# Turning x tiles 2 to 15 on VectorE from a blocked load, instead of on TensorE

## The chip, the cores and the metric
The kernel runs on one core of a Trainium2 chip. The metric is the device time of one launch in microseconds (us), the median of several runs; lower is better. The five engines are TensorE (PE: matmuls, with PEld for its weight loads), VectorE (DVE), ScalarE (ACT), GpSimd (POOL) and SyncE (SP), which here only issues DMAs. They run side by side and meet at semaphores. Each of them takes its own instructions strictly in the order in which they are written.

## What is computed
Two blocks follow one another on x, of shape (8, 256, 1024) in fp32, that is 16 tiles of 128 tokens by 1024 features:

```python
x = x + ffn0(cond0(x, lang_ids))     # cond0: x @ W0.T + 2 * top-2-gated LoRA (8 experts, rank 16)
                                     # ffn0:  top-1-routed LoRA of cond0's output (8 experts, rank 16)
x = x + ffn1(cond1(x, slot_ids))     # cond1: x @ W1.T + b1 + 2 * LoRA of the slot of each batch
                                     # ffn1:  h @ Wb.T + b_base + 2 * top-2-gated LoRA (8 experts)
```

The kernel never forms the inner activations of the dense products. It folds the weights ahead of time: C0 (1024 x 272) holds all that the first block needs of x, and M = W1.T Wb.T + I (with the routers and LoRA factors of the second block beside it) holds the dense part of the second. Products run in fp32r with each operand split in a high and a low part, so that one product is three matmuls (hi*hi, lo*hi, hi*lo), which the helper `three` issues.

## The kernel before
Up to about 181 us of its trace the kernel prepares: weights are loaded, turned on TensorE, split by ScalarE (high part) and VectorE (low part), and multiplied into C0, D0 and M. The last product there is `m_chunk(K // 2 - 1, 1, 2)`; `m_done` reaches 3 * K when it ends. Only then may `x1T`, `xT_main` and `x1_sums` be written, since they share SBUF with the weights that it reads.

Then come eight slots, b = 0 to 7. Slot b computes the output of tiles m = 2b and m + 1 and, in the same stretch of TensorE's program, the first block for tiles a = 2b + 2 and a + 1 (where there are any). For a tile t of the first block:
- x is loaded (`load_x`: one DMA of 128 rows of 4 KB into `xin`), turned by eight TensorE transposes into two PSUM banks (`turn_x_main`), and split out of PSUM by `xT_part`: ScalarE writes `xThi`, VectorE writes `xTlo`, each in two instructions of 128 x 512.
- `small0(t)` multiplies xT with C0: 24 matmuls of 272 columns. It waits for `xT_lo`, the last of the four splits.
- VectorE's `gates0` works out the top-2 gates and writes `hg`; TensorE turns it (`turn_small(hg_ready, ...)`), ScalarE and VectorE split it, `add_lora0` adds the LoRA. `top1` and `wh` do the same for the router of ffn0. `ffn0(q, g, bank)` multiplies the last factor for both tiles in four quarters of 512 columns.
- `x1_add` forms x1 = ffn0 + x for a quarter: one VectorE add of the bank and `xTlo`, a second one of that sum and `xThi`, into `x1_sums`. `x1T_part` (in the vector program: `split`) splits the quarter into `x1Thi` and `x1Tlo`.

The output of tiles m and m + 1 is 48 "main" steps of three matmuls (x1T by M, 392 columns), which `main_to(n)` advances to step n; between them stand, at steps chosen by hand, the small transposes, `small0`, `add_lora0`, `ffn0`, `lora` and `turn_x_main`. In slot 0 every count of `main_to` is 3 later (`late = 3`). Tiles n = 2b + 4 and n + 1, which the next slot's first block takes, are loaded and turned in slot b: `turn_x_main(n, 0, ...)` after step 40, `turn_x_main(n + 1, 1, ...)` between `lora(m + 1, 1)` and the last `lora(m + 1, 2)`. The next slot begins with `small0(n)`. Slots 0 to 5 have such an n.

VectorE's order at the end of a slot is: `gates1(m + 1)` with the last quarter's add in it, `split(1)`, `wzT_part(m + 1)` (the low part of the turned gates of ffn1, which waits for a TensorE transpose at step 44 and ScalarE's copy of it), `split(2)`, `split(3)`, `xT_part(n)`, `xT_part(n + 1)`, `as_part`. Tiles 0 and 1 are turned during the preparation (`xin_first`, `XT_FIRST`). Tile 2 is turned near its end (`x2_early` into the banks `XT_EARLY`), tile 3 in slot 0, after `adapter(m)`. The slots run unrolled for b = 0, 5, 6, 7 and in a hardware loop for b = 1 to 4.

Of the kernel before, what the change touches and what calls it, by code (L numbers as in the profile page):

```python
# [5 lines left out]
P = 128  # L6
F32 = mybir.dt.float32
# [16 lines left out]
def adaln_ffn(nc, x, lang_ids, slot_ids, W0, Wr0, A0c, B0, route_w, A0f, Bw, W1, b1, lora_As, lora_Bs,  # L24
# [30 lines left out]
    with ctx:  # L55
# [31 lines left out]
        wzThi, wzTlo = sb("wzThi", [P, P], F32R), sb("wzTlo", [P, P], F32R)  # L87

        def gate_tiles(n):
# [18 lines left out]
        with ExitStack() as before_m:  # L108
            sb("below_b_acc", [P, (K - 1) * MW + R], where=before_m)
            b_acc = sb("b_acc", [P, MC], where=before_m)  # L110
            sb("below_x2", [P, (K - 1) * MW + R], where=before_m)
            x2_early = sb("x2_early", [P, D], where=before_m)
        Mhi = sb("Mhi", [P, K, MW], F32R)
# [62 lines left out]
        whT_hi, whT_lo = sem("whT_hi"), sem("whT_lo")  # L176
        x1w_done, x1_half, x1_sum = sem("x1w_done"), sem("x1_half"), sem("x1_sum")
        m_ident, x2_in = sem("m_ident"), sem("x2_in")
        x1T_hi, x1T_lo = sem("x1T_hi"), sem("x1T_lo")
# [89 lines left out]

        XT_BANKS = [(big[1], big[2]), (big[0], big[1])]  # L270
        XT_FIRST = [(pm[0], pm[1]), (pm[2], pm[0])]
        XT_EARLY = (p0, pt)

# [8 lines left out]
        def half_tiles(t, half, h):  # L282
            return t[:, :].rearrange("p (k c) -> p k c", k=K)[:, 4 * h:4 * h + 4, half * P:(half + 1) * P]

        def wait_earlier(eng, s, n):

            if not isinstance(n, int) or n > 0:
                eng.wait_ge(s, n)
# [3 lines left out]
        def _(sp):  # L292
            sp.dma_start(a0f[:, :], A0f.rearrange("e r d -> (e r) d")).then_inc(a0f_in, 16)
            sp.dma_start(routers[:, 1, :], route_w).then_inc(r0_in, 16)
            w0v = W0.rearrange("(p j) i -> p j i", j=K)

            def load_b(raw, src, s):
# [49 lines left out]
            sp.wait_ge(fe_stored, 32)  # L347
            sp.dma_start(x2_early[:, :], xf[2 * P:3 * P, :]).then_inc(x2_in, 16)
            sp.wait_ge(acc_step, 1)
# [28 lines left out]
            def load_x(t, turn):  # L378
                sp.dma_start(xin[turn][:, :], xf[bass.ds(t * P, P), :]).then_inc(x_in[turn], 16)

# [26 lines left out]
            def slot_dmas(b, last, more_x):  # L407
                def store(half):
                    sp.wait_ge(y_ready, b * 6 + half * 3 + 3)
                    sp.dma_start(outf[bass.ds(b * 2 * P + half * P, P), :], ybuf[:, :]).then_inc(y_out, 16)  # L410

                if not last:
                    load_as(b + 1, True)
                store(0)
                if last:
                    for c, (y0, n) in enumerate(Y_OF):
                        sp.wait_ge(y_ready, (NT - 1) * 3 + c + 1)
                        sp.dma_start(outf[(NT - 1) * P:NT * P, y0:y0 + n], ybuf[:, y0:y0 + n]).then_inc(y_out, 16)
                    return
                sp.wait_ge(z1_done, b * 2 + 2)  # L420
                load_e(b + 1)
                store(1)
                load_f(b + 1)
                if more_x:
                    for half in range(2):
                        sp.wait_ge(tx_done, b * 4 + 10 + half * 2)
                        load_x(b * 2 + 6 + half, half)

            sp.wait_ge(tx_done, 8)
            load_x(5, 1)  # L430
# [38 lines left out]
        def _(act):  # L469
# [31 lines left out]

            def xT_part(t, half, xT, at, guard):
                if guard:
                    act.wait_ge(p0_done, t - 1)
                    act.wait_ge(x1_sum, (t - half) * 2)
# [4 lines left out]
            xT_part(0, 0, xT_first, XT_FIRST[0], False)  # L510
            act.wait_ge(d0w_done, 1)
# [59 lines left out]
            copy_units(NEF + 8, units_second[NEF - NU1 + 8:NEF - NU1 + 10])  # L571
            xT_part(1, 1, xT_first, XT_FIRST[1], False)
            whT_part(0, 0)
# [41 lines left out]
            for g in range(4):  # L615
                if g == 2:
                    xT_part(2, 0, xT_main, XT_EARLY, False)
                if g == 0:
# [6 lines left out]
            def slot(b, turn, has_a, has_n, first=False):  # L625
# [5 lines left out]
                if first:  # L631
                    xT_part(a + 1, 1, xT_main, XT_BANKS[1], False)
                exp1(m)
# [17 lines left out]
                if has_a:  # L651
                    x1T_part(q, 1 - turn, 3, quarter(x1_sums, 3))
                if has_n:
                    xT_part(n, 0, xT_main, XT_BANKS[0], True)
                wzT_part(m + 1)
                y_part(m + 1, 0)
                y_part(m + 1, 1)
                if has_n:
                    xT_part(n + 1, 1, xT_main, XT_BANKS[1], True)
                if has_a:  # L660
# [12 lines left out]
        def _(dve):  # L673
# [39 lines left out]
            def xT_part(t, half, xT, at):  # L713
                for h in range(2):
                    dve.wait_ge(xT_hi, t * 2 + h + 1)
                    lo(half_tiles(xT[1], half, h), at[h].rearrange("p (k c) -> p k c", k=4),
                       half_tiles(xT[0], half, h)).then_inc(xT_lo, 1)

            xT_part(0, 0, xT_first, XT_FIRST[0])
# [97 lines left out]

            def x1_add(q, g, bank, xT, sums):

                dve.wait_ge(x1w_done, q * 4 + g + 1)  # L820
                wait_earlier(dve, x1T_hi, q * 4 + g - 3)
                dve.tensor_tensor(quarter(sums, g), bank, quarter(xT[1], g).bitcast(F32), ALU.add).then_inc(x1_half, 1)  # L822
                dve.wait_ge(x1_half, q * 4 + g + 1)
                dve.tensor_tensor(quarter(sums, g), quarter(sums, g), quarter(xT[0], g).bitcast(F32), ALU.add)\  # L824
                   .then_inc(x1_sum, 1)

# [52 lines left out]
            for g in range(4):  # L879
                x1_add(0, g, X1W_FIRST[g], xT_first, xin_first)  # L880
            dve.wait_ge(bcol_ready, 1)
# [43 lines left out]
            dve.wait_ge(fe_stored, 64)  # L925
            keep_m(K // 2 - 1, 1, (0, 1))
            for g in range(4):
                if g == 2:
                    xT_part(2, 0, xT_main, XT_EARLY)
                x1T_part(0, 0, g, quarter(wraw[2 + g // 2], g % 2))  # L930
# [4 lines left out]
            def slot(b, turn, has_a, has_n, first=False):  # L935
                m, a, n, q = b * 2, b * 2 + 2, b * 2 + 4, b + 1

                def add(g):
                    x1_add(q, g, X1W_BANKS[g], xT_main, x1_sums)

# [7 lines left out]
                if has_a:  # L948
                    top1(a)
                    if first:  # L950
                        xT_part(a + 1, 1, xT_main, XT_BANKS[1])
                    gates1(m, lambda: whT_part(a, 0))
# [20 lines left out]
                if has_n:  # L973
                    xT_part(n, 0, xT_main, XT_BANKS[0])
                    xT_part(n + 1, 1, xT_main, XT_BANKS[1])
                if has_a:
# [11 lines left out]
        def _(pe):  # L988
# [154 lines left out]
            m_chunk(K // 2 - 1, 1, 0)  # L1143
            pe.wait_ge(x2_in, 16)
            pe.wait_ge(unit_lo, NU2 + 2)
            turn_x(x2_early, XT_EARLY)
            pe.wait_ge(acc_step, 1 + 2 * K)
# [10 lines left out]
            pe.wait_ge(bias_step, 3)  # L1158

            def turn_x_main(t, half, nth, waits):  # L1160

                pe.wait_ge(x_in[half], nth * 16)
                for h in range(2):
                    if waits:
                        pe.wait_ge(*waits[h])
                    for k in range(4):
                        ins = pe.transpose(rows(XT_BANKS[half][h], k), rows(xin[half], 4 * h + k), ident[:, :])  # L1167
                    ins.then_inc(tx_done, 1)


            def slot(b, turn, has_a, has_n, first=False):
# [41 lines left out]
                if not first:  # L1213
                    if has_a:
                        small0(a, 0, xT_main)
                    pe.wait_ge(x1T_lo, b * 4 + 4)
                pe.wait_ge(as_lo, b + 1)
                if first:
                    main_to(0)
                    small0(a, 0, xT_main)  # L1220
                main_to(7)
                if has_a:
# [7 lines left out]
                adapter(m)  # L1230
                if first:
                    turn_x_main(a + 1, 1, 1, None)
                main_to(14)
# [31 lines left out]
                if has_a:  # L1265
                    pe.wait_ge(x1_half, q * 4 + 1)
                    ffn0(q, 3, X1W_BANKS[3])
                main_to(35)
                adapter(m + 1)
                main_to(40)  # L1270
                if has_n:
                    turn_x_main(n, 0, b + 1, [(x1_half, q * 4 + 2), (x1_half, q * 4 + 3)])
                main_to(44 if has_n else 46)
# [4 lines left out]
                lora(m + 1, 1)  # L1278
                if has_n:
                    turn_x_main(n + 1, 1, b + 2, [(x1_half, q * 4 + 4), (xT_lo, n * 2 + 1)])  # L1280
                main_to(48)
# [32 lines left out]
```

## Time and profile before
| what | value |
|---|---|
| time, median of 3 runs | 510.89 us (510.64 to 512.52) |
| span of the profiled execution, first to last instruction | 509.9 us |
| PE, PEld busy | 497.2 us (98%), 475.4 us (93%) |
| DVE busy | 269.8 us (53%) |
| ACT, POOL busy | 135.9 us (27%), 9.5 us (2%) |
| mean granted TensorE clock | 0.997 |
| DMA | 40.22 MB, 79 GB/s over the span, 23.6% of the 16 engines |

The profile is of one execution. Its time as a run is not listed apart from its span; the span is 1.0 us under the median of the runs; that is taken as the part of a launch that lies around its first and last instruction. Busy shares are over the whole span. PE's 98% says that there are few gaps in its own stream, which is one program in a fixed order.

### The profile page before, as it was taken

To read this page: it belongs to the slowest core of one execution; us is meant where nothing else is said; L and a number is where in the kernel's file an instruction comes from. 1 tells how busy PE (TensorE), PEld (TensorE's weight loads), DVE (VectorE), ACT (ScalarE), POOL (GpSimd) and SP (SyncE) were. 2 spreads that over 40 slices of the span, in tenths; PEclk is the share of its full clock that TensorE was granted. 3 is DMA by queue.
4 is the path that set the end of the run, shared out by engine and by line. 5 is a ranking of instruction groups with operands and counts; after the bars stand their busy time and mean duration, and the time that the engine had idled before them with its cause. 6 is when DMAs were issued, how large, how long until landed. Compare 5 with 4: busy or idle time off the path is not lost.

```text
span 509.9 us, 8653 instructions
## 1 busy us (share of the span) xinstructions
PE 497.2 (98%) x3119; PEld 475.4 (93%) x3119; DVE 269.8 (53%) x839; ACT 135.9 (27%) x300; POOL 9.5 (2%) x18
## 2 busy tenths in 40 slices
PE   5999999999999989999999999999999999999997
PEld 4977899999999889999999999999999999999997
DVE  3655865444448355465384475466548438446211
ACT  4454620111111332241141132223124113222111
POOL 2040000000000000000000000000000000000000
PEclk9998999999999999999999999999999999999999
DMA  7984722311111131113104104012210410201111
GB/s 236 343 266 154 210 91 84 125 41 42 41 41 47 43 102 46 42 43 105 42 5 144 42 3 145 0 43 65 79 41 2 146 42 3 62 1 45 57 42 41
DMA packets 30397, 40.22 MB, mean 79 GB/s; under 512 B 10487, under 2 KB 22529, under 8 KB 30238
## 3 DMA queue, kind: packets, MB, share of 16 engines
q1 hardware_dynamic: 30094, 39.25, 23.6%
q0 software_dynamic: 272, 0.56, 0.4%
q8 instruction: 19, 0.31, 0.3%
q14 instruction: 12, 0.10, 0.1%
HBM read 28.64 MB, written 11.16 MB: 78 GB/s over the span
## 4 chain that ended last, share of the span: by engine, by line
PE 95%; DMA 2%; DVE 1%; ACT 1%; issue 0%; SPq 0%; POOL 0%; DVEq 0%; ACTq 0%
PE banks L1002 28%; PE banks L1004 27%; PE banks L1003 27%; PE banks L1016 3%; PE banks L997 3%; PE banks L1167 2%; PE banks L1200 1%; DMA wraw<-in_L_cond_W_dram 1%; PE banks L1051 1%; DMA routers<-in_L_ffn_W_router_dram 1%; PE banks L1025 1%; PE banks L1151 0%; PE banks L1205 0%; DVE ws_lo L676 0%; PE banks L1210 0%
## 5 line engine op out<-in xcount | busy, mean ns | idle before, releaser
L1002 PE MATMUL banks<-Mhi,x1Thi 128*128 128x392 f32 x384 | 138.0, 359 | 2.0 <-DVE x1Tlo L676 1.5
L1003 PE MATMUL banks<-Mlo,x1Thi 128*128 128x392 f32 x384 | 130.6, 340 | 0.0
L1004 PE MATMUL banks<-Mhi,x1Tlo 128*128 128x392 f32 x384 | 130.5, 340 | 0.0
L1002 PEld LDWEIGHTS banks<-Mhi,x1Thi 128*128 128x128 f32 x384 | 72.3, 188 | 4.5 <-issue 2.5
L1002 PE MATMUL banks<-WbThi,ws_hi 128*128 128x392 f32 (+2 forms) x216 | 74.7, 346 | 0.0
L1004 PE MATMUL banks<-WbThi,ws_lo 128*128 128x392 f32 (+2 forms) x216 | 73.2, 339 | 0.0
L1003 PE MATMUL banks<-WbTlo,ws_hi 128*128 128x392 f32 (+2 forms) x216 | 73.0, 338 | 0.0
L1003 PEld LDWEIGHTS banks<-Mlo,x1Thi 128*128 128x128 f32 x384 | 72.5, 189 | 0.0
L1004 PEld LDWEIGHTS banks<-Mhi,x1Tlo 128*128 128x128 f32 x384 | 72.2, 188 | 0.0
L1004 PEld LDWEIGHTS banks<-WbThi,ws_lo 128*128 128x128 f32 x216 | 40.7, 188 | 3.2
L1003 PEld LDWEIGHTS banks<-WbTlo,ws_hi 128*128 128x128 f32 x216 | 40.7, 188 | 3.1
L1002 PEld LDWEIGHTS banks<-WbThi,ws_hi 128*128 128x128 f32 x216 | 40.6, 188 | 3.0
L544 ACT ACTIVATE ybuf<-banks 128x392 f32<-128x392 f32 (+1 forms) x48 | 21.9, 456 | 46.2 <-PE banks L1200 46.1
L1002 PE MATMUL banks<-C0hi,xThi 128*128 128x272 f32 x112 | 32.5, 290 | 0.0
L1004 PE MATMUL banks<-C0hi,xTlo 128*128 128x272 f32 x112 | 32.3, 288 | 0.0
L1003 PE MATMUL banks<-C0lo,xThi 128*128 128x272 f32 x112 | 32.2, 287 | 0.0
L596 ACT ACTIVATE Mhi<-banks 128x392 f32 (+5 forms) x24 | 10.3, 495 | 80.4 <-DVE banks L905 60.0
L478 ACT ACTIVATE x1Thi<-x_sums 128x512 fp32r<-128x512 f32 x28 | 17.7, 632 | 42.1 <-DVE x_sums L824 42.1
L676 DVE SCALAR_TENSOR_TENSOR Mlo<-banks,Mhi 128x392 f32 (+8 forms) x30 | 15.4, 554 | 18.2 <-ACT Mhi L596 14.4
L822 DVE TENSOR_TENSOR x_sums<-banks,xTlo 128x512 f32<-128x512 f32 x28 | 19.3, 689 | 8.7 <-PE banks L1004 8.2
L1002 PEld LDWEIGHTS banks<-C0hi,xThi 128*128 128x128 f32 x112 | 21.0, 188 | 0.4 <-DVE xTlo L676 0.4
L1003 PEld LDWEIGHTS banks<-C0lo,xThi 128*128 128x128 f32 x112 | 21.1, 188 | 0.0
(186 smaller groups left out, 796.7 us busy)
## 6 DMA issues: line engine op xcount, KB each, us to landing
wraw<-in_L_cond_W_dram SPq DMA_DIRECT2D x16, 512.0 KB, 4.4
out_dram<-ybuf SPq DMA_DIRECT2D x15, 512.0 KB, 3.1
xin<-in_x_dram SPq DMA_DIRECT2D x13, 512.0 KB, 4.3
wraw<-in_L_ffn_W_base_dram SPq DMA_DIRECT2D x8, 512.0 KB, 6.5
xin_first<-in_x_dram SPq DMA_DIRECT2D x1, 1024.0 KB, 9.2
x1T_dram<-xin_first SPq DMA_DIRECT2D x1, 1024.0 KB, 3.9
wraw<-x1T_dram SPq DMA_DIRECT2D x2, 512.0 KB, 3.5
Fbuf<-fe_hi_dram SPq DMA_DIRECT2D x16, 64.0 KB
```

What stands on the lines that cost most here:

```text
L478: act.activation(dst, src, ACT.Copy).then_inc(ready, 1)
L544: act.activation(ybuf[:, y0:y0 + n], pm[c][:, PART - n:PART], ACT.Copy).then_inc(y_ready, 1)
L596: act.activation(Mhi[:, bass.ds(i * 2 + par, 1), R + c0:R + c0 + n], m_psum(M_BANKS[par], c).unsqueeze(1), ACT.Copy).then_inc(m_hi, 1)
L676: return dve.scalar_tensor_tensor(out=out_, in0=src, scalar=scale, in1=hi.bitcast(F32), op0=ALU.mult, op1=ALU.subtract)
L822: dve.tensor_tensor(quarter(sums, g), bank, quarter(xT[1], g).bitcast(F32), ALU.add).then_inc(x1_half, 1)
L997: ins = pe.transpose(unit_bank(q)[:, col:col + width], src, ident[0:kp, 0:kp])
L1002: pe.matmul(out_, l[0], r[0], start=start, stop=False, **kw)
L1003: pe.matmul(out_, l[0], r[1], start=False, stop=False, **kw)
L1004: return pe.matmul(out_, l[1], r[0], start=False, stop=stop, **kw)
L1016: ins = pe.matmul(banks[:, k, 0:2 * RC], w, R0T[:, j, :], start=j == 0 and n == 0, stop=j == K - 1 and n == 1)
L1025: ins = pe.transpose(rows(at[h], k), rows(src, 4 * h + k), ident[:, :])
L1167: ins = pe.transpose(rows(XT_BANKS[half][h], k), rows(xin[half], 4 * h + k), ident[:, :])
```

## The change
Tiles 2 to 15 of x are no longer turned by TensorE. Their load is four DMAs of 32 partitions each (`load_blocks`), which put the 32 x 32 blocks of every 128 x 128 tile at the mirrored place, in pieces of 32 fp32 (128 bytes); one VectorE `transpose` of 128 x 1024 then turns each 32 x 32 block in its place and writes the turned tile into its half of `x1_sums` (`turn_x`). ScalarE and VectorE split it from there (`xT_turned`) instead of from PSUM. Since `x1_sums` now holds turned x, `x1_add` adds the ffn0 bank to it in one instruction where it used two.

Where things stand: in every slot that has n, VectorE waits for the last `x1T_lo`, turns n and n + 1 behind `split(3)`, and only then comes `xT_turned(n)` and `xT_turned(n + 1)`. ScalarE takes `wzT_part(m + 1)` ahead of `xT_turned(n)`. Tile 2 is turned on VectorE after `m_done` reaches 3 * K, ahead of the splits of x1T; tile 3 in slot 0 behind `top1(a)`. TensorE's slot 0 runs `main_to(7)` (ten steps) ahead of `small0(2)`, where it ran `main_to(0)` (three steps). `x2_early` gets a place of its own, and the scratch of software DMAs is set to 8192 bytes.

```diff
+            def load_blocks(tile, t, s):
+                src = block_rows(t)
+                for j in range(NJ):
+                    sp.dma_start(tile[j * BLK:(j + 1) * BLK, :].rearrange("r (k i c) -> r k i c", k=K, c=BLK), src[j])\
+                      .then_inc(s, 16)
 ...
+        def block_rows(t):
+            return xf[bass.ds(t * P, P), :].rearrange("(i r) (k j c) -> j r k i c", r=BLK, j=NJ, c=BLK)
 ...
             def load_x(t, turn):
-                sp.dma_start(xin[turn][:, :], xf[bass.ds(t * P, P), :]).then_inc(x_in[turn], 16)
+                load_blocks(xin[turn], t, x_in[turn])
 ...
                     for half in range(2):
-                        sp.wait_ge(tx_done, b * 4 + 10 + half * 2)
+                        sp.wait_ge(x_turned, b * 2 + 3 + half)
                         load_x(b * 2 + 6 + half, half)
 ...  (scalar)
+            def xT_turned(t, half, guard):
+                if guard:
+                    act.wait_ge(p0_done, t - 1)
+                for h in range(2):
+                    hi_half(x_turned, t - 1, half_tiles(xT_main[0], half, h), half_tiles(x1_sums, half, h), xT_hi)
 ...
-                if has_n:
-                    xT_part(n, 0, xT_main, XT_BANKS[0], True)
                 wzT_part(m + 1)
+                if has_n:
+                    xT_turned(n, 0, True)
 ...  (vector)
+            def turn_x(t, half, src, s, n):
+                dve.wait_ge(s, n)
+                dve.transpose(half_of(x1_sums, half), src[:, :].rearrange("p (k c) -> p k c", k=K)).then_inc(x_turned, 1)
+            def xT_turned(t, half):
+                for h in range(2):
+                    dve.wait_ge(xT_hi, t * 2 + h + 1)
+                    lo(half_tiles(xT_main[1], half, h), half_tiles(x1_sums, half, h),
+                       half_tiles(xT_main[0], half, h)).then_inc(xT_lo, 1)
 ...
+            def x1_add(q, g, bank):
+                dve.wait_ge(x1w_done, q * 4 + g + 1)
+                dve.tensor_tensor(quarter(x1_sums, g), bank, quarter(x1_sums, g), ALU.add).then_inc(x1_sum, 1)
 ...
+            dve.wait_ge(m_done, 3 * K)
+            turn_x(2, 0, x2_early, x2_in, 64)
             for g in range(4):
                 if g == 2:
-                    xT_part(2, 0, xT_main, XT_EARLY)
+                    xT_turned(2, 0)
                 x1T_part(0, 0, g, quarter(wraw[2 + g // 2], g % 2))
 ...
                     if first:
-                        xT_part(a + 1, 1, xT_main, XT_BANKS[1])
+                        turn_x(a + 1, 1, xin[1], x_in[1], 64)
+                        xT_turned(a + 1, 1)
 ...
                 if has_n:
-                    xT_part(n, 0, xT_main, XT_BANKS[0])
-                    xT_part(n + 1, 1, xT_main, XT_BANKS[1])
+                    dve.wait_ge(x1T_lo, q * 4 + 4)
+                    turn_x(n, 0, xin[0], x_in[0], b * 64 + 64)
+                    turn_x(n + 1, 1, xin[1], x_in[1], b * 64 + 128)
+                    xT_turned(n, 0)
+                    xT_turned(n + 1, 1)
 ...  (tensor)
-            turn_x(x2_early, XT_EARLY)
 ...
+                main_to(7)
                 if first:
-                    main_to(0)
                     small0(a, 0, xT_main)
-                main_to(7)
 ...
-                if first:
-                    turn_x_main(a + 1, 1, 1, None)
 ...
-                main_to(40)
-                if has_n:
-                    turn_x_main(n, 0, b + 1, [(x1_half, q * 4 + 2), (x1_half, q * 4 + 3)])
 ...
-                if has_n:
-                    turn_x_main(n + 1, 1, b + 2, [(x1_half, q * 4 + 4), (xT_lo, n * 2 + 1)])
```

## Rows read from the trace of the kernel before

**Rows 1.** The page, the chain that ended last, its shares by engine
```profile
PE 95%; DMA 2%; DVE 1%; ACT 1%; issue 0%; SPq 0%; POOL 0%; DVEq 0%; ACTq 0%
```

**Rows 2.** Waits of TensorE: who for whom, us in total, times, longest
```profile
PE banks L997 <- DMA routers<-in_L_ffn_route_w_dram: 4.8, 1, 4.8
PE banks L1002 <- DVE x1Tlo L676: 1.5, 1, 1.5
```

**Rows 3.** The chain in order of time (start, us, what): eight transposes of one tile
```profile
170.06 0.87 PE banks L1025 x8
...
302.33 0.87 PE banks L1167 x8
```

**Rows 4.** VectorE's groups by shape: busy us, mean ns, idle before
```profile
L824 DVE TENSOR_TENSOR x_sums<-x_sums,xThi 128x512 f32<-128x512 f32 x28 | 19.4, 692 | 1.0
L676 DVE SCALAR_TENSOR_TENSOR ws_lo<-wraw,ws_hi 128x1024 fp32r<-128x1024 f32 x12 | 14.7, 1225 | 4.2 <-ACT ws_hi L486 3.4 <-ACT ws_hi L582 0.5
```

**Rows 5.** Timeline of TensorE where slot 2 ends (start, us, what)
```profile
305.19 0.27 PE L1051 MATMUL banks<-ident,wz 128*128 128x128 f32 x1
...
310.19 0.29 PE L1002 MATMUL banks<-C0hi,xThi 128*128 128x272 f32 x1
```

**Rows 6.** Timeline of VectorE in the same stretch
```profile
305.87 0.29 DVE L676 SCALAR_TENSOR_TENSOR wzTlo<-banks,wzThi 128x128 fp32r<-128x128 f32 x1 [0.69 <-ACT wzThi L478]
306.07 1.28 DVE L676 SCALAR_TENSOR_TENSOR x1Tlo<-x_sums,x1Thi 128x512 fp32r<-128x512 f32 x2
```

**Rows 7.** Timeline of TensorE in slot 0 and at its end
```profile
182.83 0.41 PE L1002 MATMUL banks<-Mhi,x1Thi 128*128 128x392 f32 x1 [1.53 <-DVE x1Tlo L676]
...
184.54 0.39 PE L1002 MATMUL banks<-C0hi,xThi 128*128 128x272 f32 x1
...
191.40 0.27 PE L1051 MATMUL banks<-ident,hg 128*128 128x128 f32 x1
...
197.32 0.39 PE L1002 MATMUL banks<-C0hi,xThi 128*128 128x272 f32 x1
...
222.45 0.27 PE L1051 MATMUL banks<-ident,wz 128*128 128x128 f32 x1
...
226.49 0.29 PE L1002 MATMUL banks<-C0hi,xThi 128*128 128x272 f32 x1
```

**Rows 8.** Timelines of VectorE and ScalarE in slot 0
```profile
181.99 1.29 DVE L676 SCALAR_TENSOR_TENSOR x1Tlo<-wraw,x1Thi 128x512 fp32r<-128x512 f32 x2 [2.17 <-ACT x1Thi L478]
...
189.92 0.29 DVE L733 TENSOR_TENSOR hg<-banks,gc 128x128 f32<-128x128 f32 x1
...
194.41 0.29 DVE L733 TENSOR_TENSOR wh<-banks,gt 128x128 f32<-128x128 f32 x1
195.98 1.29 DVE L676 SCALAR_TENSOR_TENSOR xTlo<-banks,xThi 128x512 fp32r<-128x512 f32 x2 [1.27 <-ACT xThi L478]
...
223.34 1.28 DVE L676 SCALAR_TENSOR_TENSOR x1Tlo<-x_sums,x1Thi 128x512 fp32r<-128x512 f32 x2
...
181.33 1.15 ACT L478 ACTIVATE x1Thi<-wraw 128x512 fp32r<-128x512 f32 x2 [2.23 <-PE banks L1004]
...
195.35 1.09 ACT L478 ACTIVATE xThi<-banks 128x512 fp32r<-128x512 f32 x2 [1.31 <-PE banks L1167]
```

**Rows 9.** DMA issues: operation, count, KB each, median us to landing
```profile
xin<-in_x_dram SPq DMA_DIRECT2D x13, 512.0 KB, 4.3
...
bwraw<-in_L_cond_lora_Bs_dram SPq DMA_DIRECT2D x8, 64.0 KB, 2.9
...
asraw<-in_L_cond_lora_As_dram SPq DMA_DIRECT2D x8, 64.0 KB, 3.5
```

**Rows 10.** TensorE's first adapter matmul, and the queue's first Ebuf load
```profile
194.64 0.23 PE L1210 MATMUL banks<-Ebuf,hsT 96*128 96x136 f32 x1
...
182.38 0.33 SPq L364 DMA_DIRECT2D Ebuf<-fe_hi_dram  x1
```

**Rows 11.** Busy time by stretch (PE, PEld, DVE, ACT, POOL), then PEclk, DMA share, GB/s
```profile
44.00:47.00 3.00, 3.00 (x17) 2.89 (x16) 1.83 (x4) 1.30 (x3) 0.00 (x0) 0.57 0.06 25
```

More of the change, by code:

```diff
@@ L87, in adaln_ffn @@
         wzThi, wzTlo = sb("wzThi", [P, P], F32R), sb("wzTlo", [P, P], F32R)
+        x2_early = sb("x2_early", [P, D])
         def gate_tiles(n):
@@ L110, in adaln_ffn @@
             b_acc = sb("b_acc", [P, MC], where=before_m)
-            sb("below_x2", [P, (K - 1) * MW + R], where=before_m)
-            x2_early = sb("x2_early", [P, D], where=before_m)
         Mhi = sb("Mhi", [P, K, MW], F32R)
@@ L177, in adaln_ffn @@
         x1w_done, x1_half, x1_sum = sem("x1w_done"), sem("x1_half"), sem("x1_sum")
+        x_turned = sem("x_turned")
         m_ident, x2_in = sem("m_ident"), sem("x2_in")
@@ L268, in adaln_ffn @@
         c0_sums = [t[:, 0:4 * RC].rearrange("p (k c) -> p k c", k=4) for t in (a0f, b1_j)]
-        XT_BANKS = [(big[1], big[2]), (big[0], big[1])]
         XT_FIRST = [(pm[0], pm[1]), (pm[2], pm[0])]
-        XT_EARLY = (p0, pt)
+        BLK = 32
+        NJ = P // BLK
         X1W_BANKS, X1W_FIRST = [big[0], big[1], big[2], big[0]], [big[0], big[1], p0, pt]
@@ L283, in half_tiles, with half_of @@
             return t[:, :].rearrange("p (k c) -> p k c", k=K)[:, 4 * h:4 * h + 4, half * P:(half + 1) * P]
+        def block_rows(t):
+            return xf[bass.ds(t * P, P), :].rearrange("(i r) (k j c) -> j r k i c", r=BLK, j=NJ, c=BLK)
+        def half_of(t, half):
+            return t[:, :].rearrange("p (k c) -> p k c", k=K)[:, :, half * P:(half + 1) * P]
         def wait_earlier(eng, s, n):
@@ L347, in _ @@
             sp.wait_ge(fe_stored, 32)
-            sp.dma_start(x2_early[:, :], xf[2 * P:3 * P, :]).then_inc(x2_in, 16)
+            load_blocks(x2_early, 2, x2_in)
             sp.wait_ge(acc_step, 1)
@@ L425, in slot_dmas @@
                     for half in range(2):
-                        sp.wait_ge(tx_done, b * 4 + 10 + half * 2)
+                        sp.wait_ge(x_turned, b * 2 + 3 + half)
                         load_x(b * 2 + 6 + half, half)
-            sp.wait_ge(tx_done, 8)
+            sp.wait_ge(x_turned, 2)
             load_x(5, 1)
@@ L500, in _, with xT_part @@
                 act.activation(C0hi[:, 4 * g:4 * g + 4, ER + E:C0C], c0_sums[g], ACT.Copy).then_inc(c0_hi, 1)
[L502 to L505, printed above, removed]
+            def xT_part(t, half, xT, at):
                 for h in range(2):
@@ L508, in xT_part @@
                             at[h].rearrange("p (k c) -> p k c", k=4), xT_hi)
-            xT_part(0, 0, xT_first, XT_FIRST[0], False)
+            def xT_turned(t, half, guard):
[3 more added lines that the diff above has]
+                    hi_half(x_turned, t - 1, half_tiles(xT_main[0], half, h), half_tiles(x1_sums, half, h), xT_hi)
+            xT_part(0, 0, xT_first, XT_FIRST[0])
             act.wait_ge(d0w_done, 1)
@@ L571, in _ @@
             copy_units(NEF + 8, units_second[NEF - NU1 + 8:NEF - NU1 + 10])
-            xT_part(1, 1, xT_first, XT_FIRST[1], False)
+            xT_part(1, 1, xT_first, XT_FIRST[1])
             whT_part(0, 0)
@@ L616, in _ @@
                 if g == 2:
-                    xT_part(2, 0, xT_main, XT_EARLY, False)
+                    xT_turned(2, 0, False)
                 if g == 0:
@@ L631, in slot @@
                 if first:
-                    xT_part(a + 1, 1, xT_main, XT_BANKS[1], False)
+                    xT_turned(a + 1, 1, False)
                 exp1(m)
@@ L652, in slot @@
                     x1T_part(q, 1 - turn, 3, quarter(x1_sums, 3))
+                wzT_part(m + 1)
                 if has_n:
-                    xT_part(n, 0, xT_main, XT_BANKS[0], True)
-                wzT_part(m + 1)
+                    xT_turned(n, 0, True)
                 y_part(m + 1, 0)
@@ L658, in slot @@
                 if has_n:
-                    xT_part(n + 1, 1, xT_main, XT_BANKS[1], True)
+                    xT_turned(n + 1, 1, True)
                 if has_a:
@@ L816, in wzT_part, with x1_first @@
                 lo(wzTlo[:, :], pt_wz, wzThi[:, :]).then_inc(wzT_lo, 1)
-            def x1_add(q, g, bank, xT, sums):
-                dve.wait_ge(x1w_done, q * 4 + g + 1)
-                wait_earlier(dve, x1T_hi, q * 4 + g - 3)
+            def x1_first(g, bank, xT, sums):
+                dve.wait_ge(x1w_done, g + 1)
                 dve.tensor_tensor(quarter(sums, g), bank, quarter(xT[1], g).bitcast(F32), ALU.add).then_inc(x1_half, 1)
-                dve.wait_ge(x1_half, q * 4 + g + 1)
+                dve.wait_ge(x1_half, g + 1)
                 dve.tensor_tensor(quarter(sums, g), quarter(sums, g), quarter(xT[0], g).bitcast(F32), ALU.add)\
                    .then_inc(x1_sum, 1)
+            def x1_add(q, g, bank):
+                dve.wait_ge(x1w_done, q * 4 + g + 1)
+                dve.tensor_tensor(quarter(x1_sums, g), bank, quarter(x1_sums, g), ALU.add).then_inc(x1_sum, 1)
             def x1T_part(q, turn, g, src):
@@ L879, in _ @@
             for g in range(4):
-                x1_add(0, g, X1W_FIRST[g], xT_first, xin_first)
+                x1_first(g, X1W_FIRST[g], xT_first, xin_first)
             dve.wait_ge(bcol_ready, 1)
@@ L938, in add @@
                 def add(g):
-                    x1_add(q, g, X1W_BANKS[g], xT_main, x1_sums)
+                    x1_add(q, g, X1W_BANKS[g])
                 def split(g):
@@ L1143, in _ @@
             m_chunk(K // 2 - 1, 1, 0)
-            pe.wait_ge(x2_in, 16)
             pe.wait_ge(unit_lo, NU2 + 2)
-            turn_x(x2_early, XT_EARLY)
             pe.wait_ge(acc_step, 1 + 2 * K)
@@ L1158, in _ @@
             pe.wait_ge(bias_step, 3)
[L1160 to L1168, printed above, removed]
             def slot(b, turn, has_a, has_n, first=False):
@@ L1265, in slot @@
                 if has_a:
-                    pe.wait_ge(x1_half, q * 4 + 1)
+                    pe.wait_ge(x1_sum, q * 4 + 1)
                     ffn0(q, 3, X1W_BANKS[3])
@@ L1302 @@
     from concourse.bass_utils import run_bass_kernel_spmd as _run
-    nc = _bacc.Bacc("TRN2", target_bir_lowering=False, num_devices=1)
+    nc = _bacc.Bacc("TRN2", target_bir_lowering=False, num_devices=1, dynamic_dma_scratch_size=8192)
     arrays, args = {}, []
```

## The prediction
> **What bounds the kernel now.** I read the shares of the chain that ended last first: PE has 95% of it [rows 1]. The list of TensorE's waits says what the rest is: 4.8 us at the start for a DMA, and 1.5 us where the slots begin, for VectorE's first x1Tlo [rows 2]; none of the others reaches 1 us, and in the slots there is almost none. So a microsecond of work taken from TensorE is a microsecond of time, if what TensorE waits for next is ready that much earlier. That is the whole question here, and the timelines of TensorE and VectorE at the two kinds of place where turned x is used answer it: the end of a slot [rows 5, 6] and slot 0 [rows 7, 8].
>
> **What is removed from TensorE.** Eight transposes of one tile take 0.87 to 0.88 us of the chain [rows 3]. Fourteen tiles: one before the slots (tile 2), one inside slot 0 (tile 3), two at the end of each of slots 0 to 5. 14 x 0.875 = 12.2 us. If nothing came late, the time would be 510.9 - 12.2 = 498.7.
>
> **What VectorE's transpose costs (T).** No row shows this operation. The nearest is VectorE's other work on 128 x 1024 in fp32, from SBUF to SBUF: 1.225 us [rows 4]. I take T = 1.22. Ends: were two columns handled in the time of one, it would be near the 0.69 of a 128 x 512 operation [rows 4]; were it half as fast, 2 x 1.225 = 2.45. I take the middle because a transpose moves as many columns as that row, and nothing in the trace shows VectorE working faster than one column in about 1.2 ns on fp32.
> The Trainium skill, "VectorE: DVE Perf Modes", section "The three transpose paths", gives 311 ns for a 128 x 128 bf16 block turned by VectorE and 390 ns on TensorE, which reads as a point in the change's favour. Eight blocks in instructions of their own would be 2.49 us by it, an estimate. This trace has TensorE at 0.87 for all eight blocks, pipelined, so the measurement is against it, and no run so far shows the VectorE side.
>
> **What VectorE is spared.** 28 second adds of 0.69 us go [rows 4], 19.4 us, and 14 transposes of 1.22, 17.1 us, come: its sum hardly moves. But the adds end before the point from which its tail at a slot's end is counted (next part), so they shorten nothing that TensorE waits for.
>
> **The end of a steady slot (slots 1 to 5).** TensorE turns wz at 305.19 and starts small0 of the next slot at 310.19 [rows 5]. One set of transposes (n) lies before the first and one (n + 1) between them. After: wz at 304.31, and small0 could start at 308.44. VectorE's tail hangs on wz: wzTlo starts 0.68 after it and the two splits take their places 0.20 later, 1.28 together [rows 5, 6]. The adds gone, VectorE reaches wzTlo earlier, but stands there. So: wzTlo 304.99, splits 305.19 to 306.47. Now two transposes come in front of xTlo: following operations overlap by about 0.08 (306.07 starts before 305.87 + 0.29 ends), so 306.50 + 2 x 1.22 - 0.08 - 0.08 = 308.78, then the pair of xTlo, 1.28 as the pair of x1Tlo, 310.06. ScalarE's two xThi are made during the second transpose. TensorE starts 0.1 later, 310.16: it waits 1.72, and the slot is as long as before (310.16 against 310.19). The 1.75 us saved per slot are lost whole. Five slots: 5 x 1.72 = 8.6 us of waits.
>
> **The end of slot 0.** Here TensorE had 4.04 us from wz (222.45) to small0 (226.49) [rows 7], of which 0.88 goes: 3.16. VectorE's splits end 2.17 after wz (223.34 + 1.28) [rows 8]; two transposes and xTlo bring it to 0.03 + 2.28 + 1.28 + 0.1 later, 5.86. Wait: 2.7 us.
>
> **The start of slot 0.** ScalarE writes x1Thi at 181.33, as m_done comes [rows 8]. VectorE now turns tile 2 first, 181.35 to 182.57, and x1Tlo starts at about 182.5, not 181.99: 0.5 us. The third quarter of x1Tlo stands behind tile 2's two splits; TensorE now needs it at its step 4 and comes to it 0.2 early. Sum 0.7.
> Then small0(2) is moved behind ten main steps. Before, three steps ran, small0 (started 184.54) and seven steps, and hg was turned at 191.40; VectorE had hg ready at 189.92 + 0.29 = 190.21, 5.67 after the start of small0 [rows 7, 8]. Seven steps, 7 x 0.535 = 3.7 us, had covered gates0. Moved ahead, they cover nothing: small0 takes 3.1, then TensorE stands until 5.75 after its start. Wait: 2.63 us. This term holds whatever T is.
>
> **Tile 3.** Its transpose stands behind top1, whose wh ended at 194.70; before, the split ran from ScalarE's start at 195.35 to 195.98 + 1.29 = 197.27, 1.92 us, and small0(3) started at 197.32 [rows 7, 8]. After, in the same clock: transpose 194.65 to 195.87, 0.06 to ScalarE, 1.92, end 197.85, TensorE 197.95. Without the eight transposes TensorE is there at 197.32 - 0.88 = 196.44. Wait: 1.5 us.
>
> **The loads.** Four DMAs of 1024 pieces of 128 bytes stand for one of 128 rows. Bounds: the 64 KB load in 1024 pieces of 64 bytes lands after 3.5 us, the 64 KB load in long rows after 2.9 [rows 9]. The difference is 9 ns for each of an engine's 64 pieces; all of the 3.5 would be 55 ns. With 256 pieces per tile and engine that is 2.3 to 14 us. I take the low end, the difference being what pieces add, so the load stays near its 4.3 us [rows 9]. At the end of a slot two tiles have some 40 us until VectorE wants them, which covers even 2 x 14. Only the loads of tiles 3 and 4 have others queued behind them on SP's queue: Ebuf's, at 182.38, for the adapter matmul at 194.64 [rows 10], and Fbuf's. I put that at nothing.
> The Trainium skill, "DMA: Bandwidth & Descriptors", section "Specifications", asks for at least 512 bytes per transfer for full rate. It speaks against the change; the 64-byte row here shows a small cost per piece, and there is time for it.
> The scratch size and x2_early's place cost nothing: the load of tile 2 still has tens of us before m_done.
>
> **Sum.** -12.2 (transposes) + 0.7 (start) + 2.6 (gates0) + 1.5 (tile 3) + 2.7 (end of slot 0) + 8.6 (five ends) = +3.9 us. On the profiled execution: 509.9 + 3.9 = 513.8. The runs' median stands 1.0 above the span: **514.8 us**.
> T stands in the sum 14 times (start, tile 3, and twice at six ends), each on the path. So each 0.1 us of T is 1.4 us of time.
>
> **Rivals.**
> 1. *T is short* (ends not slower). At T = 0.69 the sum is 3.9 - 14 x 0.53 = -3.5: 507.4 us. It gives less than before's time from T under 1.22 - 3.9 / 14 = 0.94. For it: a transpose has one source where the row of 1.225 has two. Against: no fp32 row is faster.
> 2. *T is long.* At T = 2.45: 3.9 + 14 x 1.23 = +21: 532 us; at T = 1.6, +5 more: 520. For it: a block must be filled before it can be read out.
> 3. *The tail at a slot's end isn't what TensorE waits for*, because VectorE, spared its adds, is far enough ahead. Then the 8.6 and 2.7 vanish: 503.5 us. Against: wzTlo is bound to a TensorE transpose, not to VectorE's own load [rows 6].
> 4. *Slow pieces.* Tiles 3 and 4 are 512 pieces per engine ahead of Ebuf. Data flows from about 183.3; Ebuf must land at 194.64 + 3.3 = 197.9, with 2 us of latency: it decides from (197.9 - 2 - 183.3) / 512 = 25 ns a piece. At 55 ns TensorE would stand 512 x 0.030 = 15 us: 530 us.
> 5. *TensorE's clock falls.* After the 4.8 us wait [rows 2] a stretch of 3 us ran at a granted clock of 0.57, the lower level of 1.2 GHz being half of 2.4 [rows 11]. That costs about 1.3 us each time. The waits of 1.5 us left it at full. If the two of 2.6 to 2.7 and a few more bring it down: +1.3 to +6, some 518.
>
> **How the numbers follow.** The forecast with its terms as summed: 0.62, own range 512 to 518 (0.15 us on T, 0.1 us on each wait). T short: 0.11. T long: 0.10. The tail not late: 0.04. Slow pieces: 0.05. Clock: 0.08. About 0.5% (2.6 us) is what a measurement tells from no change: under 508.3 is faster, over 513.4 slower. Faster: most of T short and the tail, 0.13. Same: the rest of these, and a quarter of the forecast's own range, 0.22. Slower: 0.65. The range leaves out the far ends of T, slow pieces and the tail: 509 to 521.
>
> **What would show each step.** In the changed profile: VectorE's transposes as 14 of 128 x 1024 with mean T. TensorE's waits by source: for xTlo, seven (six ends and tile 3), 12.8 us in all, 1.7 at each steady end; for hg, one of 2.6; for x1Tlo 2.2. Slots 1 to 5 still 41.9 us each. The x loads' landings near 4 to 6 us. Wrong would be: slots near 40.1 us (the tail hidden), T away from 1.2, a wait for Ebuf, or a clock below 1 after 181 us.

## The result and the profile after

The changed kernel takes 518.0 us (median of 4 runs, 517.9 to 519.2) against 511.6 for the kernel before (4 runs, 510.6 to 512.5): a ratio of 1.013, 95% interval 1.011 to 1.015. It is 6.5 us slower, where 3.9 were forecast. The profiled execution has a span of 516.0 us and was a run of 517.9, so 1.9 us lie around the span, not the 1.0 that the prediction took. A clock below 1 after 181 us, which the prediction named as a sign of being wrong, is in this profile; it comes last in this section.

The list of TensorE's waits of the changed kernel (who for whom, us in total, times, longest):

```profile
PE banks L1041 <- DVE xTlo L694: 11.8, 7, 2.6
...
PE banks L1090 <- DVE hg L762: 2.4, 1, 2.4
PE banks L1041 <- DVE x1Tlo L694: 2.0, 1, 2.0
```

In [rows 2] there was only the last of the three, at 1.5. VectorE's groups by shape give the price that no row of before had (the last row is the operation from which it was taken, as in [rows 4]):

```profile
L858 DVE TENSOR_TENSOR x_sums<-banks,x_sums 128x512 f32<-128x512 f32 x28 | 19.2, 687 | 7.8 <-PE banks L1043 7.8
...
L740 DVE STREAM_TRANSPOSE x_sums<-xin 128x1024 f32<-128x1024 f32 x13 | 15.5, 1225 | 0.6
L694 DVE SCALAR_TENSOR_TENSOR ws_lo<-wraw,ws_hi 128x1024 fp32r<-128x1024 f32 x12 | 14.7, 1224 | 4.2 <-ACT ws_hi L501 3.4 <-ACT ws_hi L600 0.5
```

A transpose of 128 x 1024 takes 1.225 us, within a nanosecond of what the other operation of this size takes. The row has 13 of them; the fourteenth is tile 2's, which has another source and took 1.245.

The timeline of VectorE at the end of slot 2, which answers to [rows 6]:

```profile
310.65 0.29 DVE L694 SCALAR_TENSOR_TENSOR wzTlo<-banks,wzThi 128x128 fp32r<-128x128 f32 x1 [1.78 <-ACT wzThi L493]
310.86 1.28 DVE L694 SCALAR_TENSOR_TENSOR x1Tlo<-x_sums,x1Thi 128x512 fp32r<-128x512 f32 x2
312.27 2.37 DVE L740 STREAM_TRANSPOSE x_sums<-xin 128x1024 f32<-128x1024 f32 x2
...
314.56 2.68 DVE L694 SCALAR_TENSOR_TENSOR xTlo<-x_sums,xThi 128x512 fp32r<-128x512 f32 x4
```

and of TensorE there, which answers to [rows 5] (the two rows ahead of the last are the closing matmuls of `lora(m + 1, 1)` and `lora(m + 1, 2)`):

```profile
309.97 0.27 PE L1090 MATMUL banks<-ident,wz 128*128 128x128 f32 x1
...
312.68 0.34 PE L1226 MATMUL banks<-Fbuf,hsT 96*128 96x392 f32 x1
...
313.93 0.34 PE L1226 MATMUL banks<-Fbuf,hsT 96*128 96x392 f32 x1
315.87 0.39 PE L1041 MATMUL banks<-C0hi,xThi 128*128 128x272 f32 x1 [1.60 <-DVE xTlo L694]
```

VectorE stands idle for 1.78 us before wzTlo: that is where the spared adds went. Behind wzTlo come two splits, two transposes (2.37 together) and the pair of xTlo, and TensorE waits 1.60 for it. The row of 1.60 recurs at five slot ends with 1.5 to 1.6, and once with 2.63 at the end of slot 0.

A row's wait is counted from the modelled end of the matmul before it, and in a full stream the next matmul starts before that end. So what a wait costs is read from start to start. In the kernel before, the same stretch was:

```profile
307.88 0.34 PE L1200 MATMUL banks<-Fbuf,hsT 96*128 96x392 f32 x1
308.07 1.04 PE L1167 MATMUL banks<-ident,xin 128*128 128x128 f32 x8
...
310.01 0.34 PE L1200 MATMUL banks<-Fbuf,hsT 96*128 96x392 f32 x1
```

From one LoRA matmul to the other it took 2.13 us with the eight transposes between them, and 1.25 without: they are worth 0.88. From the last of them to small0 it was 0.18 (310.01 to 310.19) and is 1.94 (313.93 to 315.87): the row's 1.60 costs TensorE 1.76, and small0's first matmuls lose another 0.1.

The profile shows one thing more. Busy time by stretch (PE, PEld, DVE, ACT, POOL, then the granted clock of TensorE, the DMA share and GB/s):

```profile
179.40:181.40 2.00, 0.00 (x1) 0.03 (x1) 1.97 (x3) 1.84 (x4) 0.95 (x1) 1.00 0.17 28
182.00:185.00 3.00, 3.00 (x12) 3.00 (x12) 2.55 (x6) 1.29 (x3) 0.00 (x0) 0.56 1.06 158
...
230.00:233.00 3.00, 2.42 (x10) 2.42 (x11) 2.02 (x4) 1.74 (x5) 0.00 (x0) 0.53 0.14 55
```

TensorE stood still for 2.0 us at 179.4, and from 182 it ran at about half its clock (1.2 instead of 2.4 GHz) for over 3 us. The same follows the wait of 2.63 us that ended at 230.6. Before, neither place had a stretch below 1.00. After the 2.4 us wait for hg the clock stayed at 1.00.

### The profile page after: what moved, and what is told of

Its sections match the earlier page's. It is cut to its first block, busy times and chain, and to the rows that moved or that the text cites. A ratio compares the mean times of both kernels' runs of the same rounds, so it can differ in the third digit from the quotient of the medians.

```text
span 516.0 us, 8448 instructions
## 1 busy us (share of the span) xinstructions
PE 490.1 (95%) x3007; PEld 467.2 (91%) x3007; DVE 266.9 (52%) x825; ACT 135.3 (26%) x300; POOL 9.5 (2%) x18
## 4 chain that ended last, share of the span: by engine, by line
PE 88%; DVE 7%; issue 2%; DMA 1%; ACT 1%; DVEq 0%; POOL 0%; SPq 0%; ACTq 0%
PE banks L1041 26%; PE banks L1043 26%; PE banks L1042 26%; PE banks L1055 3%; PE banks L1036 3%; DVE x_sums L740 2%; DVE x1Tlo L694 2%; DVE xTlo L694 1%; PE banks L1090 1%; PE banks L1226 1%; DMA routers<-in_L_ffn_W_router_dram 1%; DMA routers<-in_L_ffn_route_w_dram 1%; PE banks L1064 0%; PE banks L1188 0%; ACT wzThi L493 0%
## 5 line engine op out<-in xcount | busy, mean ns | idle before, releaser
L1041 PE MATMUL banks<-C0hi,xThi 128*128 128x272 f32 x112 | 33.7, 301 | 11.8 <-DVE xTlo L694 11.8
L858 DVE TENSOR_TENSOR x_sums<-banks,x_sums 128x512 f32<-128x512 f32 x28 | 19.2, 687 | 7.8 <-PE banks L1043 7.8
```

The costliest lines, as they stand in the source:

```text
L858: dve.tensor_tensor(quarter(x1_sums, g), bank, quarter(x1_sums, g), ALU.add).then_inc(x1_sum, 1)
L1041: pe.matmul(out_, l[0], r[0], start=start, stop=False, **kw)
```

## The experiments

**The clock.** Two explanations stood for what the waits and the removed work leave open: the two falls of the clock, or the loads. The first run keeps TensorE at work in its waits.

```diff
+                def fill(bank, count):
+                    for i in range(count):
+                        pe.transpose(rows(bank, i % 4), ident[:, :], ident[:, :])
 ...
+                if first:
+                    fill(pm[2], 16)
                 main_to(7)
                 if first:
                     small0(a, 0, xT_main)
+                    fill(pm[2], 20)
 ...
                 main_to(15)
+                if first:
+                    fill(big[2], 10)
 ...
                 lora(m + 1, 2)
+                if has_n:
+                    fill(big[2], 20 if first else 13)
```

> The changed kernel, with TensorE given idle work in its five kinds of waits: transposes of the identity into a PSUM bank that nothing reads at that time, 0.11 us each (16 before slot 0, 20 before hg, 10 before tile 3, 20 at the end of slot 0, 13 at each of five other ends). They end before the awaited data is there, so no wait's end moves. Theory (about 3 of the 6.5 us are two falls of TensorE's clock, each after a wait): no fall inside the slots, granted clock 1.00 there, time about 3 us under the changed kernel, +3.5 us against before (1.007). Rival (the excess is the loads in pieces or longer waits): time as the changed kernel, +6.5 us (1.013).

Measured: 515.3 us, ratio 1.0083 (1.0059 to 1.0106), 2.7 us under the changed kernel. In its profile the slots run at 1.00 throughout (the same columns as above):

```profile
180.00:192.00 12.00, 11.83 (x84) 11.27 (x82) 6.37 (x19) 3.64 (x8) 0.59 (x1) 1.00 0.82 108
192.00:232.00 40.00, 38.90 (x257) 37.48 (x256) 23.82 (x82) 11.22 (x28) 0.00 (x0) 1.00 0.16 35
232.00:513.60 281.60, 277.34 (x1757) 272.87 (x1755) 138.01 (x546) 66.14 (x170) 0.00 (x0) 1.00 0.25 53
```

TensorE did 131 more transposes and was done earlier. The medians differ by 2.7 us and the profiled spans by 2.4 (516.0 and 513.6). Followed matmul by matmul, the two streams of TensorE part by 1.25 us in the first low stretch and by 1.33 in the second, and by less than 0.1 anywhere else in the slots. So a fall of the clock cost some 1.3 us here, and no wait ended earlier or later for the idle work.

**The loads alone.** In the kernel before, `load_x` and the load of x2_early become four DMAs each in pieces of 128 bytes; the TensorE transposes stay.

```diff
-                sp.dma_start(xin[turn][:, :], xf[bass.ds(t * P, P), :]).then_inc(x_in[turn], 16)
+                load_blocks(xin[turn], t, x_in[turn])
 ...
-                pe.wait_ge(x_in[half], nth * 16)
+                pe.wait_ge(x_in[half], nth * 64)
```

> The kernel before with one part of the change alone: tiles 2 to 15 are loaded in four DMAs of 1024 pieces of 128 bytes each, and still turned by TensorE (so the blocks lie in the wrong places and the output is not the reference's). Theory (there is time for the loads): no change, 0.998 to 1.003, the landings some 4 to 6 us. Rival (slow pieces delay TensorE, or the DMAs slow the engines' SBUF accesses): +1 us or more.

Measured: ratio 1.0008 (0.9982 to 1.0034). The interval alone (-0.9 to +1.7 us) doesn't exclude the rival's +1 us; the trace does. Matmul by matmul TensorE keeps the pace of the kernel before in every slot, with one step of 0.3 us at slot 0's first adapter matmul (194.57). That is where Ebuf is first read, whose load now stands behind eight issues that take 6.5 us, at 187.67 instead of 182.38 [rows 10]; that this is what the 0.3 us waited for is not shown. In the changed kernel the adapter matmul comes at 197.26 and loses nothing. The loads are as good as free here. Their row among the DMA issues, which answers to [rows 9]:

```profile
xin<-in_x_dram SPq DMA_DIRECT2D x52, 128.0 KB, 3.9
```

**The tail of a slot.** The changed kernel, with VectorE's idle time before wzTlo used.

```diff
                     split(1)
-                    wzT_part(m + 1)
                     split(2)
                     split(3)
+                    if has_n:
+                        dve.wait_ge(x1T_lo, q * 4 + 4)
+                        turn_x(n, 0, xin[0], x_in[0], b * 64 + 64)
+                    wzT_part(m + 1)
 ...
-                    turn_x(n, 0, xin[0], x_in[0], b * 64 + 64)
-                    turn_x(n + 1, 1, xin[1], x_in[1], b * 64 + 128)
                     xT_turned(n, 0)
+                    turn_x(n + 1, 1, xin[1], x_in[1], b * 64 + 128)
                     xT_turned(n + 1, 1)
```

> The changed kernel, with VectorE's order at a slot's end altered: split(2), split(3) and the transpose of tile n go ahead of wzTlo, into its idle 1.8 us, and the transpose of n + 1 goes behind the split of n. Theory (the 7.9 + 2.6 us of waits at six ends are exactly the two transposes in a tail that hangs on wzTlo): those waits fall from 10.5 us to under 1.5, and the clock's fall at the end of slot 0 goes with them; 10 to 12 us under the changed kernel, 506 to 508 (ratio to before 0.99 to 0.995). Rival (the ends are bound by something else as well, ScalarE's order or the loads): less than half of that comes, ratio above 1.002.

Measured: 507.1 us (505.1 to 509.0), ratio 0.991 (0.988 to 0.994), 11 us under the changed kernel, as expected. Its waits of TensorE:

```profile
PE banks L1091 <- DVE hg L762: 2.4, 1, 2.4
PE banks L1042 <- DVE x1Tlo L694: 2.0, 1, 2.0
PE banks L1042 <- DVE xTlo L694: 1.3, 1, 1.3
PE banks L1042 <- DVE wzTlo L694: 0.8, 1, 0.8
```

All six waits for xTlo at slot ends are gone, and with them the fall of the clock behind slot 0; the 1.3 is tile 3's. The fall behind the wait of 2.0 us at the start is still there (a clock of 0.5 from about 184.6 to 188). VectorE does the same instructions. Their order at the slot ends alone made the change slower than before.

**The order in slot 0.** The changed kernel with three steps, small0(2), and then the rest, as before.

```diff
-                main_to(7)
                 if first:
+                    main_to(0)
                     small0(a, 0, xT_main)
+                main_to(7)
```

> The changed kernel, with TensorE's slot 0 in the old order: three main steps, small0(2), seven main steps, then hg. Theory (2.4 us of wait for hg come from the ten steps put ahead of small0): that wait goes, small0 waits some 0.1 us for xTlo, and the time falls by 2.2 to 2.5 us, to about +4.2 against before (1.008). Rival (the order matters little, since a later wait takes it up): within 0.5 us of the changed kernel (1.0125).

Measured: 515.0 us, ratio 1.0065 (1.0045 to 1.0084), 3.0 us less than the changed kernel. The wait for hg is no longer in the list and no wait for tile 2's xTlo took its place (xTlo: 7 times, 11.8 us, as before). The 0.6 us beyond the wait are not assigned. Between the two profiles, matmul by matmul, the old order gives 2.7 us at hg and 1.3 more because the clock, which fell behind 184 us, did not fall at 230, although the wait of 2.6 us there was the same; and the preparation takes 1.6 back, in which the clock was low for some 10 us instead of some 3. So the clock differs between executions of nearly the same stream.

**Doubling a cost.** The changed kernel, in which VectorE turns tile n + 1 twice at six slot ends.

```diff
+                    dve.wait_ge(x_in[1], b * 64 + 128)
+                    dve.transpose(half_of(x1_sums, 1), xin[1][:, :].rearrange("p (k c) -> p k c", k=K)).then_inc(x_again, 1)
+                    dve.wait_ge(x_again, b + 1)
                     turn_x(n + 1, 1, xin[1], x_in[1], b * 64 + 128)
```

> The changed kernel with the transpose of tile n + 1 done twice at the six slot ends. Theory (each transpose there lies on the path): 6 x 1.22, with 0.1 for the wait between them, +7.3 to +8 us over the changed kernel, ratio to before 1.027 to 1.030; the waits for xTlo grow from 11.8 to some 19.5 us. Rival (VectorE has slack at the slot ends): less than 4 us more, below 1.021.

Measured: 535.2 us, ratio 1.0458 (1.0431 to 1.0486): 17.2 us over the changed kernel, more than twice what I expected. The waits at the six ends grew as expected, from 10.5 to 18.2 us (3.9 at the end of slot 0, 2.8 to 2.9 at the others), and tile 3's shrank to 0.2. For the rest I looked at the clock:

```profile
PE banks L1045 <- DVE xTlo L695: 18.5, 7, 3.9
```

```profile
225.00:232.00 7.00, 3.52 (x21) 2.84 (x19) 5.70 (x8) 2.57 (x6) 0.00 (x0) 1.00 0.00 1
232.00:237.00 5.00, 4.36 (x22) 4.37 (x23) 1.99 (x4) 1.23 (x4) 0.00 (x0) 0.66 0.44 147
...
270.00:277.00 7.00, 4.56 (x28) 4.19 (x26) 5.90 (x8) 2.77 (x7) 0.00 (x0) 1.00 0.00 1
277.00:283.00 6.00, 5.56 (x31) 5.56 (x32) 2.36 (x8) 1.33 (x4) 0.00 (x0) 0.72 0.43 133
```

With waits of 2.9 us in place of 1.6, and 3.9 in place of 2.6, the clock falls at every one of the six ends, for 3 to 7 us each. In slot 0 it fell behind the wait of 2.4 us for hg (at 195) and not behind that of 2.0, the other way round than in the changed kernel. To separate the two, the same kernel with idle work in the waits, as in the first run but with 32 transposes at the end of slot 0 and 24 at the others:

> The kernel that does the transpose of tile n + 1 twice, with idle transposes of the identity in TensorE's waits (16 before slot 0, 20 before hg, 10 before tile 3, 32 at the end of slot 0, 24 at each of five other ends, 0.11 us each). The waits end when they did. Theory (of the 17.2 us that doubling cost, 6.7 to 7.5 are the transposes and some 10 are the clock's falls that the longer waits bring): 11 to 13 us under the kernel without the idle work, 522 to 524, ratio to before 1.018 to 1.023. Rival (the doubled transposes cost more than their time for another reason): less than 4 us under it, above 1.037.

Measured: 523.5 us, ratio 1.0235 (1.0192 to 1.0278); 11.7 us under the doubled kernel, a hair above the upper end of the ratio expected. From 229 us to its end it ran at a clock of 1.00:

```profile
229.00:520.00 291.00, 287.11 (x1842) 282.37 (x1840) 147.05 (x557) 68.48 (x174) 0.00 (x0) 1.00 0.25 52
```

Against the first run (515.3), whose idle work it has with more of it at the slot ends, but with single transposes there, it is 8.2 us: six times 1.36, where a transpose and the wait between were put at 1.22 and 0.1. The two profiled spans (521.2 and 513.6) give 1.27. So with the clock held, a transpose at a slot's end costs its whole duration, and what the clock takes comes on top.

**What the removed work is worth.** The kernel before with one of every four transposes of tiles 2 to 15 kept.

```diff
-                    for k in range(4):
+                    for k in range(3, 4):
                         ins = pe.transpose(rows(XT_BANKS[half][h], k), rows(xin[half], 4 * h + k), ident[:, :])
```

> The kernel before with three of every four TensorE transposes of tiles 2 to 15 left out (84 of 112; their columns of xT keep old values, so the output is not the reference's). It measures by itself what the removed work is worth. Theory (0.11 us each, all on the chain): -9.2 us, less 0.7 us where the end of slot 0 has VectorE late: 0.982 to 0.985 of before. Rival (part of the transposes was hidden, so that the change had less to gain than 12.2 us): above 0.987.

Measured: ratio 0.9864 (0.9832 to 0.9895), 7.0 us less, short of the 8.5 expected; the interval reaches into both expectations. The trace tells them apart. Matmul by matmul, each of the 14 places where six transposes are left out brings TensorE 0.66 us forward, 0.11 for each: 9.2 us in all, as the theory had it, and none was hidden. Some 2 us of it go again in new waits for VectorE, which TensorE now reaches too early: at wz (0.3 in its longest row), at tile 3 and at the end of slot 0. The theory had only 0.7 us of such waits.

**All orders mended.** The tail as above; tile 2 turned behind two quarters of x1T; tile 3 turned behind gates0; six steps ahead of small0(2). ScalarE's split of tile 2 moves with VectorE's.

```diff
             for g in range(4):
+                if g == 2:
+                    dve.wait_ge(m_done, 3 * K)
+                    turn_x(2, 0, x2_early, x2_in, 64)
+                if g == 3:
+                    xT_turned(2, 0)
 ...
                     gates0(a, q)
+                    if first:
+                        turn_x(a + 1, 1, xin[1], x_in[1], 64)
                     hgT_part(a)
 ...
                 if first:
+                    main_to(3)
                     small0(a, 0, xT_main)
+                main_to(7)
```

> All orders mended at once. At slot ends as in the run with the tail's order altered (1.3 us or less of waits left). In slot 0: tile 2 is turned behind two quarters of x1T instead of ahead of them, TensorE runs six steps, small0, four steps; tile 3 is turned in VectorE's idle 1.9 us behind gates0. Theory: against the changed kernel 0.5 us less at the start, the hg wait 0.5 instead of 2.4, the wait for tile 3 gone (1.3); 3.5 us under the run with the tail alone, 503 to 504, ratio 0.982 to 0.987. Rival (the rest of slot 0's waits moves elsewhere): above 0.989.

Measured: 502.1 us (500.9 to 502.7), ratio 0.980 (0.978 to 0.983): 10.2 us faster than the kernel before and 16 faster than the changed one. That is 5.0 us under the run with the tail alone, where 3.5 were expected; this profile has no fall of the clock in the slots, and that one has one at 184 us. TensorE's waits in the slots:

```profile
PE banks L1044 <- DVE x1Tlo L694: 1.5, 1, 1.5
...
PE banks L1044 <- DVE wzTlo L694: 0.8, 1, 0.8
...
PE banks L1093 <- DVE hg L762: 0.3, 1, 0.3
```

With idle work in the wait of 1.5 us as well:

> The same, with 13 idle transposes of the identity (1.4 us) in TensorE's wait at the start of the slots. Theory (this wait brings the clock down for a stretch and costs some 1.6 us): 0 to 1.7 us under the same kernel without them, more where the profile of that one shows a fall at 180 us. Rival (the waits that are left don't touch the clock): equal within 0.3 us.

Measured: 501.4 us, ratio 0.980 (0.978 to 0.983). The 0.7 us between the medians are inside the spread. Neither profile has a fall of the clock inside the slots, so this pair doesn't tell the two expectations apart.

**The changed kernel again**, beside other runs of before:

> The changed kernel as it is, once more beside the kernel before, as the measure for the other runs. Both theories: ratio 1.011 to 1.015, two stretches at the lower clock inside the slots or one, at one of the longer waits.

Measured: 519.1 us, ratio 1.0137 (1.0096 to 1.0179). Its waits are the same (11.9, 2.4, 2.0), and this profile too has the clock low in two places of the slots, at the start (the stretch lies across the first two rows) and behind the end of slot 0 (the third):

```profile
178.00:186.00 8.00, 6.00 (x38) 5.71 (x37) 5.18 (x8) 3.94 (x7) 0.95 (x1) 0.92 0.38 60
186.00:230.00 44.00, 40.05 (x246) 38.62 (x245) 21.96 (x87) 8.48 (x22) 0.00 (x0) 0.98 0.28 45
230.00:240.00 10.00, 7.37 (x41) 7.30 (x41) 6.12 (x19) 3.71 (x9) 0.00 (x0) 0.83 0.46 111
```

## Why the direction came out and the size did not

**The bound and the direction: right.** TensorE's stream lost its transposes, and the waits that took their place are those named, at the places named. T was put at 1.22 and is 1.225; its rivals, short and long, fall. The rival in which the tail isn't what TensorE waits for falls by the waits of 1.5 to 2.6 us at all six ends; VectorE, spared its adds, only stands idle for longer (1.78 us) before wzTlo. The rival of slow pieces falls by the run with the loads alone.

**The terms, one by one**, forecast and measured. The measured ones come from the two profiles, before and after, by following TensorE's stream matmul by matmul from start to start; the clock's are those of the run with idle work:

| term | forecast | measured |
|---|---|---|
| five slot ends | 8.6 | 9.1 |
| end of slot 0 | 2.7 | 2.9 |
| wait for hg | 2.6 | 2.7 |
| tile 3 | 1.5 | 1.4 |
| start of the slots | 0.7 | 0.5 |
| transposes removed | -12.2 | -12.4 |
| clock | 0 | 2.6 |
| preparation, apart from the change | 0 | -1.0 |
| not assigned | 0 | 0.3 |
| sum | 3.9 | 6.1 |

The terms that the prediction worked out sum to +4.2 where it had +3.9: it had the waits and the removed work right, each within 0.5 us. The preparation's -1.0 was there at 161 us, ahead of tile 2's transposes. In the later profile of the same changed kernel TensorE came to that point 2.1 us later, and nothing shows that the change has a part in it.

**What failed is a term put at nothing: the clock.** The fifth rival had it, with a chance of 0.08, and read the profile of before so: a wait of 4.8 us is followed by a low stretch, the wait of 1.5 us is not. For the waits between, it had no row, and it took the side that costs nothing. Three forecast waits, 2.2 to 2.7 us, lay in that gap, and two of them brought the clock down, 2.6 us in all. The size per fall (1.3 us) was right.
The Trainium skill, "TensorE: Matmul & The Clock Gate", section "Why this matters for your kernels", warns only of idle gaps longer than those found to matter here. By that rule the forecast waits would cost nothing; the runs with idle work are against it.

**Second, 0.9 us of the result is the base**: the prediction set the span 1.0 us below the time of a run, from a median of other runs, and it is 1.9. With that, 513.8 + 2.2 + 1.9 is 517.9, the profiled run's time.

**What was luck.** The fifth rival names "some 518", which is the time measured, but its sum for that was the clock alone, and here 0.9 us of base and -1.0 of preparation happen to cancel. That the total came only 2.6 us above the forecast's +3.9 is in part luck too: the clock fell behind two of the three longer waits, and in the run with small0 first behind only one of the two that it has left.

## What to carry to other kernels

When work moves from the engine that bounds a kernel to one that is half idle, what counts is the other engine's order: put the moved work into the gap that precedes its next wait, not behind the chain that the bound engine waits for. Here VectorE's order at the slot ends alone was the difference between 1.3% slower and 0.9% faster; with the orders of slot 0, TensorE's among them, it is 2.0% faster. And price each new wait of TensorE twice, once by its length and once by the chance that the clock falls behind it; cheap idle matmuls in a wait show at once which part is the clock's. And read what a wait costs from start to start of the matmuls around it: its row can be 0.15 to 0.25 us short of that.

## What the runs showed of the hardware

- VectorE's transpose of 32 x 32 blocks on 128 x 1024 fp32, SBUF to SBUF, takes 1.225 us (1.20 to 1.25), the same as a two-source operation on as many columns.
- Waits of TensorE of 2.0 and 2.63 us were each followed by over 3 us at the lower clock, one of 2.44 us in the same execution was not, and those of 1.6 us never were; behind the doubled kernel's waits of 2.8 to 3.9 us all six were. In other executions it was not the same waits: the one of 2.6 us left the clock at full in the run with small0 first, and in the doubled kernel that of 2.0 did and that of 2.4 did not. So between 2.0 and 2.6 us the length doesn't decide; what else does is open.
- 4096 pieces of 128 bytes for a 512 KB tile cost at most 0.3 us of the kernel's time: each of the four DMAs landed 3.9 us after its issue (median), where the single one took 4.3. Their issue takes longer, 0.64 us each in the median instead of 0.35, and eight in a row took 6.3 us in the changed kernel (6.5 in the run with the loads alone), which puts whatever is queued behind them off by 5 us.
- Eight fp32 transposes of 128 x 128 on TensorE are worth some 0.87 us when they are removed, the time that they took in the chain; the six of eight in the run above gave 0.66.
